# Splitting the first load of an expert half and scaling its second step's rows on VectorE

## The chip, the cores and the metric

The kernel runs on one core of one Trainium2 chip. The metric is the device time of one launch in microseconds (us). Before the change it is 1599.24 us, the median of three runs.

## What is computed

The reference is one layer of three residual blocks on an input `x` of 2 sequences, 4096 tokens each, 256 wide: half of a mixture-of-experts feed-forward block (FFN), an attention block of the delta-rule kind, and half of the same FFN again, each on a layer norm of `x`.

```python
x = x + 0.5 * ffn(layernorm(x))
x = x + attention(layernorm(x))
x = x + 0.5 * ffn(layernorm(x))

def ffn(x, gate_w, w1, w2, w3):          # 8192 tokens, 8 experts, width 256, hidden 128
    scores = softmax(x @ gate_w)
    top_scores, top_idx = top_k(scores, 2)
    scale = zeros((T, E)).at[arange(T)[:, None], top_idx].set(top_scores)
    xs = scale.T[:, :, None] * x[None]
    h = silu(einsum('etd,edh->eth', xs, w1)) * einsum('etd,edh->eth', xs, w3)
    return einsum('eth,ehd->etd', h, w2).sum(axis=0)
```

## The kernel before

`build` calls `ffn`, `attention` and `ffn` again. Both FFNs run the same expert code. A token goes to two experts, so the work is done in two **halves**: the first half takes every token to its best expert, the second to its second best. The tokens of a half lie in a list in device memory (`rows1`, named first_rows in the trace, then `rows2`, named second_rows), sorted by expert. A row of the first list holds the token (256 floats) and 6 floats (goal, factors, addends): 1048 bytes. A row of the second list has 256 floats more ahead of them, the token plus half of the first expert's answer (the **sum part**): 2072 bytes. The remaining 262 floats are called the **token part** here.

A half has 18 **steps** (`NSP`), numbered `start` to `end - 1`, so there are 36 steps in an FFN (`NST`) and the second half starts at step 18. A step is 4 tiles of 128 rows, each with one expert. The queues are these, and their order is the order of the code:

- SyncE (SP) loads rows: `load_rows(k)` at L360 to L368 reads four row addresses from a table in SBUF with `table_row` (L345, a TENSOR_LOAD and registers), then issues four transfers, each with an address instruction ahead of it. There are 8 row buffers `xw[k % 8]`. At step 18 it first waits until every store of the first half has landed, since those stores write the list that it now reads.
- ScalarE (ACT) in `scaled(k)` (L752) multiplies the step's rows by their factors and adds the addends, one instruction for a tile, into `xs[k % 2]` (a view of ffn_xb in the trace). `high_part(k)` (L759) rounds the turned rows, `silu(k)` is L764, `high_hidden(k)` L769.
- TensorE (PE) turns the rows with `turn_rows(k)` (L457, 8 matmuls), multiplies them with two expert matrices in `up(k)` (L468, 24 matmuls), turns the hidden values (`turn_hidden`, L481) and multiplies down (`down`, L491).
- VectorE (DVE) casts the goals (`goals(k)`, L652), makes the low part of the turned rows (`low_part(k)`, L657), multiplies the hidden values (`hidden`, L662), makes their low part (`low_hidden`, L667), and adds half of the answer (`results`, L673).
- GpSimd (POOL) stores the rows of a step by indirect transfers, one for a tile (`put`, L829).

`up(k)` needs both parts of the turned rows of its step, and stands on TensorE's queue behind `turn_rows(start + 1)` in the first step of a half. What comes before the first `silu` of a half is called its **head** here. There are four heads: H1 and H2 in the first FFN (starting at 133.88 and 260.27 us), H3 and H4 in the second (1336.16 and 1462.25 us).

Of the kernel before, what the change touches and what calls it, by code (L numbers as in the profile page):

```python
# [6 lines left out]
P = 128  # L7
# [202 lines left out]
def ffn(nc, name, src, rows1, rows2, sums, kept, fresh, first_stage):  # L210
# [13 lines left out]
    with ctx:  # L224
# [3 lines left out]
        def sem(n):  # L228
            return kept.semaphore(f"{name}_{n}")

        def sems(n, k):
            return [sem(f"{n}{j}") for j in range(k)]
# [70 lines left out]
        def pt(n, shape):  # L303
# [19 lines left out]
        scattered = sems("scattered", 4)  # L323
        tab_step, tab_ready, filled = sem("tab_step"), sem("tab_ready"), sems("filled", 2)
        row_loaded, stored, xs_ready = sems("row_loaded", NW), sems("stored", NW), sem("xs_ready")
        (to_ready, tr_done, xhi_ready, xlo_ready, up_done, sil_ready, hid_ready, hT_done, hhi_ready, hlo_ready,
         down_done, y_ready) = (sem(n) for n in (
             "to_ready", "tr_done", "xhi_ready", "xlo_ready", "up_done", "sil_ready", "hid_ready", "hT_done",
# [22 lines left out]
        def _(sp):  # L351
# [4 lines left out]
            def load_rows(k):  # L356

                if k >= NW:
                    sp.wait_ge(stored[k % NW], 16 * TPB * (k // NW))
                if k == NSP:  # L360
                    for b in range(NW):
                        sp.wait_ge(stored[b], 16 * TPB * ((NSP + NW - 1 - b) // NW))
                    sp.wait_ge(filled[1], 16 * E)
                for j, r in enumerate(table_row(k, 1, mybir.EngineType.SP, NROWS - P)):
                    if k < NSP:
                        sp.dma_start(xw[k % NW][:, j, DM:], rows1[bass.ds(r, P)]).then_inc(row_loaded[k % NW], 16)  # L366
                    else:
                        sp.dma_start(xw[k % NW][:, j], rows2[bass.ds(r, P)]).then_inc(row_loaded[k % NW], 16)  # L368
# [38 lines left out]
        def _(pe):  # L407
# [39 lines left out]
                          start=False, stop=True, skip_group_check=True).then_inc(pos_done, 1)  # L447

            def turn_rows(k):
                pe.wait_ge(xs_ready, k + 1)  # L450
                if k == 0 and first_stage:
                    pe.wait_ge(xT_ready, 2 * NG)
                wait(pe, xhi_ready, k)
                wait(pe, xlo_ready, k)
                for j in range(TPB):
                    for q in range(KC):
                        last = pe.transpose(tr[:, q, j * P:(j + 1) * P], xs[:, k % 2, j, q * P:(q + 1) * P], ident[:])  # L457
                last.then_inc(tr_done, 1)
# [74 lines left out]
        def _(dve):  # L533
# [114 lines left out]
            def goals(k):  # L648
# [2 lines left out]
                wait(dve, stored[k % NW], 16 * TPB * (k // NW))  # L651
                dve.tensor_copy(to[:, k % NW], xw[k % NW][:, :, 2 * DM + 5 if k < NSP else 2 * DM]).then_inc(to_ready, 1)  # L652

            def low_part(k):
                dve.wait_ge(xhi_ready, k + 1)
                wait(dve, up_done, k - 1)
                dve.tensor_tensor(xlo[:, k % 2], tr, xhi[:, k % 2].bitcast(F32), ALU.subtract).then_inc(xlo_ready, 1)  # L657
# [11 lines left out]
            def results(k):  # L669
                for h in range(2):  # L670
                    two = slice(2 * h, 2 * h + 2)
                    dve.wait_ge(down_done, 2 * k + h + 1)
                    dve.scalar_tensor_tensor(xw[k % NW][:, two, 0:DM], yb[:, two], 0.5,  # L673
                                             xw[k % NW][:, two, DM:2 * DM] if k < NSP else xw[k % NW][:, two, 0:DM],
                                             ALU.mult, ALU.add).then_inc(y_ready, 1)
# [32 lines left out]
                split_low(NG - 1)  # L708

            for start, end in HALVES:  # L710
                goals(start)
                low_part(start)
                goals(start + 1)
# [14 lines left out]
        def _(act):  # L728
# [59 lines left out]
            for start, end in HALVES:  # L788
                scaled(start)
                high_part(start)  # L790
                scaled(start + 1)
                high_part(start + 1)
                scaled(start + 2)
                for k in range(start, end):
                    silu(k)
                    if k + 2 < end:
# [1524 lines left out]
```

## Time and profile before

| | us |
|---|---|
| three runs | 1593.64, 1599.24, 1599.90 |
| their median | 1599.24 |
| the profiled execution's own time | 1593.92 |
| its span, from the first to the last instruction | 1592.2 |

| engine | busy us | share of the span |
|---|---|---|
| TensorE matmul | 1325.0 | 83% |
| TensorE weight load | 1241.4 | 78% |
| VectorE | 1119.1 | 70% |
| GpSimd | 998.5 | 63% |
| ScalarE | 918.2 | 58% |

The profile is of one execution. Busy shares are means over stages with different limits: the steady part of a half keeps TensorE busy all the time, and a head leaves it idle. So a change to the heads is read in the four heads, in the timeline and in the chain of waits, and not in the shares.

### The profile page before, as it was taken

To read this page: it belongs to the slowest core of one execution; us is meant where nothing else is said; L and a number is where in the kernel's file an instruction comes from. 1 tells how busy PE (TensorE), PEld (TensorE's weight loads), DVE (VectorE), ACT (ScalarE), POOL (GpSimd) and SP (SyncE) were. 2 spreads that over 40 slices of the span, in tenths; PEclk is the share of its full clock that TensorE was granted. 3 is DMA by queue.
4 is the path that set the end of the run, shared out by engine and by line. 5 is a ranking of instruction groups with operands and counts; after the bars stand their busy time and mean duration, and the time that the engine had idled before them with its cause. 6 is when DMAs were issued, how large, how long until landed. Compare 5 with 4: busy or idle time off the path is not lost. (4 is left out here: it accounts for less than half of the span.)

```text
span 1592.2 us, 36649 instructions
## 1 busy us (share of the span) xinstructions
PE 1325.0 (83%) x11688; PEld 1241.4 (78%) x11688; DVE 1119.1 (70%) x2788; ACT 918.2 (58%) x1853; POOL 998.5 (63%) x1812
## 2 busy tenths in 40 slices
PE   7773994994589999999999999999999841995996
PEld 7663994994478888888888888888888741994996
DVE  6574772673768788879888888797887534673674
ACT  2123772771356676767676767676767423772773
POOL 4772673575366676777776867877768532575466
PEclk8556996998789999999999999999999965997999
DMA  7437976672011212132222231322222245875792
GB/s 212 154 108 190 312 256 223 233 252 69 11 30 39 51 46 75 40 74 76 63 67 58 62 77 35 79 72 67 68 56 62 62 143 157 267 265 190 251 291 75
DMA packets 224024, 195.88 MB, mean 123 GB/s; under 512 B 105556, under 2 KB 186714, under 8 KB 223840
## 3 DMA queue, kind: packets, MB, share of 16 engines
q1 hardware_dynamic: 190560, 117.21, 26.8%
q0 software_dynamic: 24576, 67.94, 11.7%
q10 hardware_dynamic: 8704, 8.39, 1.8%
q8 instruction: 102, 1.67, 0.5%
q14 instruction: 82, 0.67, 0.1%
HBM read 103.68 MB, written 96.10 MB: 125 GB/s over the span
## 5 line engine op out<-in xcount | busy, mean ns | idle before, releaser
L1557 DVE SCALAR_TENSOR_TENSOR raw_w<-attn_raw,taps,raw_w 128x256 f32<-128x256 f32 x576 | 249.0, 491 | 58.6 <-ACT raw_w L1928 58.6
L468 PE MATMUL ffn_both<-ws,ffn_xhi 128*128 x1152 | 204.3, 289 | 0.4
L468 PEld LDWEIGHTS ffn_both<-ws,ffn_xhi 128*128 128x128 f32 x1152 | 164.8, 192 | 2.8 <-issue 2.8
L457 PE MATMUL ffn_both<-ident,ffn_xb 128*128 128x128 f32 x576 | 82.0, 290 | 94.7 <-ACT ffn_xb L752 94.7
L2210 POOL TENSOR_TENSOR attn_inv<-attn_inv,attn_term 64x14 f32<-64x14 f32 (+6 forms) x448 | 136.5, 305 | 35.1
L2207 POOL TENSOR_TENSOR attn_term<-attn_small,attn_inv 64x14 f32<-64x14 f32 (+6 forms) x448 | 131.1, 293 | 32.6
L1199 PE MATMUL attn_fr<-attn_xhi,wqkv 128*128 128x256 f32 x768 | 148.0, 295 | 2.5 <-DVE attn_xlo L1537 1.6
L457 PEld LDWEIGHTS ffn_both<-ident,ffn_xb 128*128 128x128 f32 x576 | 70.1, 150 | 97.1 <-ACT ffn_xb L752 76.9
L491 PE MATMUL ffn_yb<-ws,ffn_hhi 128*128 x576 | 119.9, 292 | 6.2 <-DVE ffn_hlo L667 6.2
L1199 PEld LDWEIGHTS attn_fr<-attn_xhi,wqkv 128*128 128x128 f32 x768 | 112.5, 193 | 14.1 <-issue 10.6
L829 POOL DMA_INDIRECT second_rows<-ffn_more_rows,ffn_to x64 | 63.1, 986 | 85.3 <-DVE ffn_to L652 69.3
L468 PE MATMUL ffn_both<-ws,ffn_xlo 128*128 x576 | 116.1, 283 | 0.0
L657 DVE TENSOR_TENSOR ffn_xlo<-ffn_both,ffn_xhi 128x1024 fp32r<-128x1024 f32 x72 | 87.7, 1218 | 37.0 <-ACT ffn_xhi L759 36.8
L662 DVE TENSOR_TENSOR ffn_hid<-ffn_both,ffn_sil 128x512 f32<-128x512 f32 x72 | 49.8, 691 | 88.8 <-ACT ffn_sil L764 88.8
L752 ACT ACTIVATE ffn_xb<-ffn_more_rows 128x256 f32<-128x256 f32 x120 | 62.1, 591 | 79.0 <-DMA ffn_more_rows<-first_rows 44.0
L491 PEld LDWEIGHTS ffn_yb<-ws,ffn_hhi 128*128 128x128 f32 x576 | 94.5, 191 | 7.2 <-issue 7.2
L764 ACT ACTIVATE ffn_sil<-ffn_both 128x512 f32<-128x512 f32 x72 | 43.0, 597 | 91.0 <-PE ffn_both L468 91.0
L759 ACT ACTIVATE ffn_xhi<-ffn_both 128x1024 fp32r<-128x1024 f32 x72 | 73.9, 1026 | 34.0 <-PE ffn_both L457 34.0
L468 PEld LDWEIGHTS ffn_both<-ws,ffn_xlo 128*128 128x128 f32 x576 | 90.0, 191 | 0.0
L2150 POOL DMA_INDIRECT first_rows<-attn_xg,attn_slots x64 | 66.8, 1043 | 36.6 <-issue 17.1
L818 POOL DMA_INDIRECT first_rows<-ffn_xb,ffn_slots x64 | 65.0, 1016 | 36.8 <-DVE ffn_xb L642 18.9
L1928 ACT ACTIVATE raw_w<-attn_raw,taps 128x256 f32<-128x256 f32 x192 | 86.7, 498 | 1.6
(317 smaller groups left out, 4051.1 us busy)
## 6 DMA issues: line engine op xcount, KB each, us to landing
ffn_more_rows<-second_rows SPq DMA_DIRECT2D x56, 259.0 KB
ffn_xb<-second_rows SPq DMA_DIRECT2D x48, 259.0 KB
raw_w<-second_rows SPq DMA_DIRECT2D x40, 259.0 KB
ffn_more_rows<-first_rows SPq DMA_DIRECT2D x64, 131.0 KB
ffn_xb<-in_L_attn_x_dram SPq DMA_DIRECT2D x8, 1024.0 KB, 5.9
attn_xin<-x_after_first ACTq DMA_DIRECT2D x32, 256.0 KB, 2.7
attn_xres<-x_after_first SPq DMA_DIRECT2D x32, 256.0 KB, 3.0
x_after_attention<-attn_xres SPq DMA_DIRECT2D x32, 256.0 KB
```

What stands on the lines that cost most here:

```text
L457: last = pe.transpose(tr[:, q, j * P:(j + 1) * P], xs[:, k % 2, j, q * P:(q + 1) * P], ident[:])
L468: last = pe.matmul(hp[:, j, :], (xhi, xlo)[b][:, k % 2, q, j * P:(j + 1) * P], ws[:, bass.ds(experts[j], 1), a, q].rearrange("p o d -> p ( ...
L491: last = pe.matmul(yb[:, j, :], (hhi, hlo)[b][:, k % 2, j * P:(j + 1) * P], ws[:, bass.ds(experts[j], 1), a, 2].rearrange("p o d -> p (o d)"),
L657: dve.tensor_tensor(xlo[:, k % 2], tr, xhi[:, k % 2].bitcast(F32), ALU.subtract).then_inc(xlo_ready, 1)
L759: act.activation(xhi[:, k % 2], tr, ACT.Copy).then_inc(xhi_ready, 1)
L818: pool.indirect_dma_start(out=rows1, out_offset=bass.IndirectOffsetOnAxis(ap=slots[:, m % 2, j:j + 1], axis=0), in_=xb[:, m % 4, j, :], in ...
L1199: last = pe.matmul(out, w[:, a, q, col], (xhi, xlo)[b][:, q, :], skip_group_check=True, start=(start and k == 0 and q == 0), stop=(k == 2 ...
L1557: dve.scalar_tensor_tensor(acc[:, j, r], raw[:, j, r, :, tap:tap + P], taps[:, j, r, tap:tap + 1], acc[:, j, r], ALU.mult, ALU.add)\
L1928: act.activation(acc[:, j, r], raw[:, j, r, :, 0:P], ACT.Copy, scale=taps[:, j, r, 0:1])\
L2150: pool.indirect_dma_start(out=rows1, out_offset=bass.IndirectOffsetOnAxis(ap=slots[:, j:j + 1], axis=0), in_=xg[:, j, :], in_offset=None). ...
L2207: pool.tensor_tensor(term[:, 0:k, 0:j], n[:, j + 1:, j:j + 1].broadcast_to([BP, k, j]), v[:, j:j + 1, 0:j].broadcast_to([BP, k, j]), ALU.m ...
L2210: pool.tensor_tensor(v[:, j + 1:, 0:j], v[:, j + 1:, 0:j], term[:, 0:k, 0:j], ALU.subtract)\
```

## The change

It touches `ffn` alone, and so both FFNs.

1. ScalarE no longer scales the rows of the second step of a half (`start + 1`). It scales those of `start` and, behind `high_part(start)`, those of `start + 2`.
2. VectorE scales them, in the new `second_scaled`, ahead of `goals(start)` and `low_part(start)` on its queue. TensorE waits for the new semaphore `xs_second` in that step.
3. At step 18 SyncE reads its addresses before it waits for the stores, and loads the rows in two parts: the four token parts first, then the four sum parts with a semaphore of their own (`sum_loaded`). The first `results` of the second half waits for that one.

```diff
@@ load_rows(k), SyncE
                 if k >= NW:
                     sp.wait_ge(stored[k % NW], 16 * TPB * (k // NW))
+                places = table_row(k, 1, mybir.EngineType.SP, NROWS - P)
                 if k == NSP:
+                    sp.wait_ge(filled[1], 16 * E)
                     for b in range(NW):
                         sp.wait_ge(stored[b], 16 * TPB * ((NSP + NW - 1 - b) // NW))
-                    sp.wait_ge(filled[1], 16 * E)
-                for j, r in enumerate(table_row(k, 1, mybir.EngineType.SP, NROWS - P)):
+                    for j, r in enumerate(places):
+                        sp.dma_start(xw[k % NW][:, j, DM:], rows2[bass.ds(r, P), DM:]).then_inc(row_loaded[k % NW], 16)
+                    for j, r in enumerate(places):
+                        sp.dma_start(xw[k % NW][:, j, 0:DM], rows2[bass.ds(r, P), 0:DM]).then_inc(sum_loaded, 16)
+                    return
+                for j, r in enumerate(places):
@@ turn_rows(k), TensorE
-                pe.wait_ge(xs_ready, k + 1)
+                if k in (1, NSP + 1):
+                    pe.wait_ge(xs_second, 1 if k == 1 else 2)
+                else:
+                    pe.wait_ge(xs_ready, k + 1 - (k > 1) - (k > NSP + 1))
@@ VectorE
+            def second_scaled(k):
+                dve.wait_ge(row_loaded[k % NW], 16 * TPB * (k // NW + 1))
+                if k == 1 and first_stage:
+                    wait_scattered(dve)
+                wait(dve, tr_done, k - 1)
+                c = 2 * DM + 1 if k < NSP else 2 * DM + 3
+                for j in range(TPB):
+                    row = xw[k % NW][:, j]
+                    last = dve.tensor_scalar(xs[:, k % 2, j], row[:, DM:2 * DM], row[:, c:c + 1], row[:, c + 1:c + 2],
+                                             ALU.mult, ALU.add)
+                last.then_inc(xs_second, 1)
@@ results(k), VectorE
                     dve.wait_ge(down_done, 2 * k + h + 1)
+                    if k == NSP and h == 0:
+                        dve.wait_ge(sum_loaded, 16 * TPB)
@@ the loop over the halves, VectorE
             for start, end in HALVES:
+                second_scaled(start + 1)
                 goals(start)
                 low_part(start)
@@ the loop over the halves, ScalarE
                 scaled(start)
                 high_part(start)
-                scaled(start + 1)
+                scaled(start + 2)
                 high_part(start + 1)
-                scaled(start + 2)
```

SyncE's queue at step 18 of the first FFN, where the second half starts. Before:

```order
L345 TENSOR_LOAD tab [waits ffn1_stored4,ffn1_stored5,ffn1_stored3,ffn1_stored6,ffn1_stored2,ffn1_stored7,ffn1_stored1,ffn1_filled1,ffn1_stored0]
L368 ISA
L368 DMA ffn_more_rows<-second_rows 128x518
...
L345 TENSOR_LOAD tab [waits ffn1_stored3]
...
L368 DMA raw_w<-second_rows 128x518
```

After (each DMA row stands for four, with an ISA or REGISTER_ALU row ahead of each):

```order
L346 TENSOR_LOAD tab [waits ffn1_stored2]
L367 ISA [waits ffn1_stored4,ffn1_stored3,ffn1_stored5,ffn1_stored2,ffn1_stored6,ffn1_stored1,ffn1_stored7,ffn1_stored0,ffn1_filled1]
L367 DMA ffn_more_rows<-second_rows 128x262
...
L369 REGISTER_ALU
L369 DMA ffn_more_rows<-second_rows 128x256
...
L346 TENSOR_LOAD tab [waits ffn1_stored3]
...
L375 DMA raw_w<-second_rows 128x518
```

The address read moved ahead of the wait for the stores, and four more transfers stand ahead of the loads of step 19 (into raw_w).

ScalarE's queue in the head of that half, before:

```order
L752 ACTIVATE ffn_xb<-ffn_more_rows 128x256 [waits ffn1_tr_done,ffn1_row_loaded2]
L759 ACTIVATE ffn_xhi<-ffn_both 128x1024 [waits ffn1_up_done,ffn1_tr_done]
L752 ACTIVATE ffn_xb<-raw_w 128x256 [waits ffn1_tr_done,ffn1_row_loaded3]
...
L759 ACTIVATE ffn_xhi<-ffn_both 128x1024 [waits ffn1_up_done,ffn1_tr_done]
L752 ACTIVATE ffn_xb<-raw_w 128x256 [waits ffn1_tr_done,ffn1_row_loaded4]
```

and after:

```order
L777 ACTIVATE ffn_xb<-ffn_more_rows 128x256 [waits ffn1_tr_done,ffn1_row_loaded2]
L784 ACTIVATE ffn_xhi<-ffn_both 128x1024 [waits ffn1_up_done,ffn1_tr_done]
L777 ACTIVATE ffn_xb<-raw_w 128x256 [waits ffn1_tr_done,ffn1_row_loaded4]
...
L784 ACTIVATE ffn_xhi<-ffn_both 128x1024 [waits ffn1_up_done,ffn1_tr_done]
L789 ACTIVATE ffn_sil<-ffn_both 128x512 [waits ffn1_hid_ready,ffn1_up_done]
```

The scaling of step 19 (row_loaded3) left this queue, and the second rounding now stands behind the scaling of step 20 (row_loaded4).

VectorE's queue in the first head, after the change; before it, the same rows stood without the two of L672:

```order
L672 TENSOR_SCALAR ffn_xb<-ffn_more_rows 128x256 [waits ffn1_scattered2,ffn1_scattered1,ffn1_scattered3,ffn1_scattered0,ffn1_row_loaded1]
L672 TENSOR_SCALAR ffn_xb<-ffn_more_rows 128x256 x3
L662 CAST ffn_to<-ffn_more_rows 128x4 [waits ffn1_row_loaded0]
L679 TENSOR_TENSOR ffn_xlo<-ffn_both,ffn_xhi 128x1024 [waits ffn1_xhi_ready]
L662 CAST ffn_to<-ffn_more_rows 128x4 [waits ffn1_row_loaded1]
L679 TENSOR_TENSOR ffn_xlo<-ffn_both,ffn_xhi 128x1024 [waits ffn1_xhi_ready]
```

The low part of the first step (the first L679) now stands behind four scalings that wait for the second step's rows.

## Rows read from the trace of the kernel before

**Rows 1.** Chain of waits, head H4: start us, us, what.

```profile
1459.54 2.10 DMA second_rows<-ffn_more_rows,ffn_to
1462.25 0.33 SPq L368
...
1463.80 3.72 DMA ffn_more_rows<-second_rows
...
1472.59 2.07 ACT ffn_xb L752 x4
1474.71 1.97 PE ffn_both L457 x8
1476.68 4.04 PE ffn_both L468 x24
```

**Rows 2.** Chain of waits, steady part of the last half, two steps.

```profile
1499.73 2.83 PE ffn_both L468 x24
...
1505.29 2.83 PE ffn_both L468 x24
```

**Rows 3.** Timeline of the last half, GpSimd's first store of a step.

```profile
1494.63 0.98 POOL L829 DMA_INDIRECT out_dram<-raw_w,ffn_to  x1 [0.69 <-DVE ffn_to L652]
```

**Rows 4.** Timeline, head H3 (start us, us, engine, line, operation).

```profile
1336.16 6.98 SPq L366 DMA_DIRECT2D ffn_more_rows<-first_rows  x12
...
1340.23 2.07 ACT L752 ACTIVATE ffn_xb<-ffn_more_rows 128x256 f32<-128x256 f32 x4 [23.20 <-DMA ffn_more_rows<-first_rows]
1342.36 1.97 PE L457 MATMUL ffn_both<-ident,ffn_xb 128*128 128x128 f32 x8 [29.52 <-ACT ffn_xb L752]
...
1345.42 1.22 DVE L657 TENSOR_TENSOR ffn_xlo<-ffn_both,ffn_xhi 128x1024 fp32r<-128x1024 f32 x1 [5.02 <-ACT ffn_xhi L759]
...
1349.02 0.78 PE L468 MATMUL ffn_both<-ws,ffn_xhi 128*128 x2
...
1353.88 0.60 ACT L764 ACTIVATE ffn_sil<-ffn_both 128x512 f32<-128x512 f32 x1 [0.19 <-PE ffn_both L468]
```

**Rows 5.** Timeline, head H1.

```profile
133.88 7.24 SPq L366 DMA_DIRECT2D ffn_more_rows<-first_rows  x12
137.60 2.07 ACT L752 ACTIVATE ffn_xb<-ffn_more_rows 128x256 f32<-128x256 f32 x4 [20.29 <-DMA ffn_more_rows<-first_rows]
...
142.96 1.23 DVE L657 TENSOR_TENSOR ffn_xlo<-ffn_both,ffn_xhi 128x1024 fp32r<-128x1024 f32 x1 [5.19 <-ACT ffn_xhi L759]
...
146.56 0.78 PE L468 MATMUL ffn_both<-ws,ffn_xhi 128*128 x2
...
149.89 0.40 PE L468 MATMUL ffn_both<-ws,ffn_xhi 128*128 x2
149.96 1.28 ACT L764 ACT_TABLE_LOAD   x1
```

**Rows 6.** Lines by form: VectorE, the nearest operation to the new scaling.

```profile
L1530 DVE TENSOR_SCALAR attn_xn<-attn_xin,attn_mv,attn_rstd 128x256 f32<-128x256 f32 x64 | 25.2, 433 | 1.2 <-POOL attn_rstd L2133 1.2
```

**Rows 7.** Windows (stretch, us, PE, PEld, DVE, ACT, POOL, PEclk, DMA share, GB/s).

```profile
1351.40:1353.70 2.30, 2.30 (x16) 2.30 (x16) 0.29 (x1) 2.28 (x4) 0.00 (x0) 0.67 0.81 222
...
1476.70:1478.70 2.00, 2.00 (x11) 2.00 (x11) 0.93 (x1) 1.99 (x4) 0.00 (x0) 0.50 1.05 397
...
146.90:148.90 2.00, 2.00 (x15) 2.00 (x14) 0.90 (x1) 1.95 (x4) 0.00 (x0) 0.72 0.88 264
```

**Rows 8.** Timeline, head H4: SyncE's loads of steps 19 and 20, and the low part.

```profile
1464.65 4.63 SPq L368 DMA_DIRECT2D raw_w<-second_rows  x8
...
1472.73 1.22 DVE L657 TENSOR_TENSOR ffn_xlo<-ffn_both,ffn_xhi 128x1024 fp32r<-128x1024 f32 x1 [5.02 <-ACT ffn_xhi L759]
```

**Rows 9.** Timeline, head H2.

```profile
260.27 1.94 SPq L368 DMA_DIRECT2D ffn_more_rows<-second_rows  x4
...
266.24 2.07 ACT L752 ACTIVATE ffn_xb<-ffn_more_rows 128x256 f32<-128x256 f32 x4 [17.79 <-DMA ffn_more_rows<-second_rows]
...
273.40 1.97 PE L457 MATMUL ffn_both<-ident,ffn_xb 128*128 128x128 f32 x8 [3.07 <-ACT ffn_xb L752]
```

More of the change, by code:

```diff
@@ L325, in ffn @@
         row_loaded, stored, xs_ready = sems("row_loaded", NW), sems("stored", NW), sem("xs_ready")
+        sum_loaded, xs_second = sem("sum_loaded"), sem("xs_second")
         (to_ready, tr_done, xhi_ready, xlo_ready, up_done, sil_ready, hid_ready, hT_done, hhi_ready, hlo_ready,
```

## Prediction

> **What bounds the kernel now.** I read the chain of waits first. In the steady part of a half it runs through TensorE: `up` comes back after 5.56 us, from 1499.73 to 1505.29 [rows 2]. GpSimd has room there, since it waits 0.69 us for the next step's stores [rows 3]. So a half is a head plus steps at TensorE's pace, and what a head gains reaches the end of the program.
>
> In a head the chain leaves TensorE. H4 shows it best [rows 1]: the last store lands at 1461.64 (1459.54 + 2.10), SyncE issues its first load at 1462.25, the fourth at 1463.80 lands 3.72 us later. ScalarE scales the first step's rows, TensorE turns them, ScalarE rounds them, and only at 1472.59 does ScalarE scale the second step's rows, for 2.07 us. TensorE turns these from 1474.71 for 1.97 us and starts `up` at 1476.68. But `up` of the first step had its last input when VectorE finished the low part, at 1473.95 (1472.73 + 1.22) [rows 8]. The 2.7 us between are a detour: work of the second step ahead of the first step's `up`. H3 has the same pattern, low part ready at 1346.64 and `up` from 1349.02 [rows 4], and so has H1, 144.19 and 146.56 [rows 5].
>
> **The new scaling.** It is four tensor_scalar of 128x256 f32 with two operands per partition. L1530 has that very form and takes 433 ns [rows 6], so 4 x 0.433 = 1.7 us, in place of ScalarE's 2.07 us. It stands on VectorE ahead of the first low part, so that one waits until the second step's rows have landed and been scaled.
>
> The Trainium skill speaks of a shorter time: by "VectorE: DVE Perf Modes", section on the perf-mode tier table, a tensor_scalar on fp32 in SBUF runs at twice the plain rate. By that page an estimate is 0.3 us for each of the four, and the sum would be 10.5 us and not 9.5 us. The row above does not agree with it for this form, and I go by the row.
>
> **H3 and H1, first halves (loads unchanged).** In H3 twelve loads are issued in 6.98 us [rows 4], in three groups of four. A group takes 1.9 us [rows 9], so groups start 2.55 us apart. The first is landed at 1340.23, the second then at 1342.8. Scaled, it is ready at 1344.5, just as the first turning ends (1344.33). TensorE turns it until 1346.5. The low part is not delayed: its input is there at 1345.42, and it is ready at 1346.64. So `up` starts at 1346.7, 2.3 us sooner than 1349.02. In H1 a group comes every 2.65 us (12 in 7.24 us) after 137.60: the second lands at 140.25, is ready at 142.0 and turned by 144.0; low part at 144.19; `up` from 144.3, 2.3 us sooner than 146.56 [rows 5].
>
> Two things add to that. First, in H1 the table load for silu lasts until 151.24, while `up` was over at 150.29 (149.89 + 0.40) [rows 5]: 1 us of waiting. ScalarE now comes to the table load sooner. Third group landed at 142.9, scaled 142.95 to 145.0, second rounding to 146.0, table load to 147.3: 3.9 us sooner. Second, TensorE's clock. In the heads it was granted 0.5 (the 1.2 GHz level) and rose to the 2.4 GHz level within `up`: 0.67 on the mean over 1351.40 to 1353.70, 0.72 over 146.90 to 148.90 [rows 7]. Before, the engine idled 3.07 us between the two turnings; now they follow each other in H1 and H3. The rise may come earlier with that, or it may come when it came, and then more of `up` is slow. 24 matmuls take 2.83 us at the high level [rows 2], and 5.1 to 5.7 us at the low one (8 turnings take 1.97 us, 0.25 each with the fill, 0.21 without it). From 1346.7, `up` in H3 ends between 1349.6 and 1351.8, against 1353.88 before: 2.1 to 4.2 us gained. I take 3.4, since TensorE is now busy for 4 us before `up`. In H1 silu comes between 147.3 (table load) and 149.4, against 151.24: 1.8 to 3.9 us, and I take 3.2.
>
> **H4 and H2, second halves.** Reading the addresses early takes the TENSOR_LOAD out from between the last landing and the first issue. The gap was 0.61 us (1461.64 to 1462.25) and an address instruction stays, so I take 0.45 us, between 0.1 and 0.6. First issue: 1461.8. Four token parts are as large as the first halves' rows, which had landed 3.72 us (H1) and 4.07 us (H3) after their first issue [rows 4, 5]. Whole rows took 5.27 us in H4 (1462.25 to 1467.52) and 5.97 us in H2 (260.27 to 266.24) [rows 1, 9]. So the first step's rows are there at 1465.7, 1.8 us sooner, and they are turned by 1469.8.
>
> But the second step's rows now stand behind eight transfers and not four. Their first issue was 2.4 us after the first step's (1462.25 to 1464.65 [rows 8]). Four more at 0.52 us each (1463.80 less 1462.25, over three) make it 4.5 us: 1466.3. Four whole rows need 5.3 to 6.0 us, so they land at 1471.6 to 1472.3. VectorE scales them until 1473.3 to 1474.0, against 1474.66 for ScalarE before. So this gains 1.4 to 0.7 us and not 2.7: the second step's rows are the **new wait**, and little of the split load's 1.8 us is left on the path. I take 1.1 in H4. In H2 the same sum (260.27 - 0.45 + 4.5 + 5.3 to 6.0, plus 1.7) gives 271.3 to 272.0, against 273.40 [rows 9]: 2.1 to 1.4 gained, and I take 1.8. The clock does as before here, since TensorE still idles some 3.5 us between the turnings.
>
> Behind the new wait stands the low part of step 18, ready at 1474.5 to 1475.2. Step 19's turning ends at 1475.3 to 1476.0, so it costs nothing. On ScalarE the second rounding stands behind the scaling of step 20. The transfers run at their limit in this stretch (DMA share 1.05, 397 GB/s [rows 7]); a step's 1.06 MB take 2.7 us, so step 20 lands by 1475.0, is scaled by 1477.1, step 19 rounded by 1478.1, its low part done by 1479.4. The second `up` needs that at about 1481.7, so 2.3 us cover it; without that cover it would cost its excess in H2 and H4. The sum parts are needed by `results` some 15 us later: nothing. In steady steps nothing changes on any engine, and GpSimd's queue is not touched.
>
> **Sum.** 3.2 (H1) + 1.8 (H2) + 3.4 (H3) + 1.1 (H4) = 9.5 us. The low ends give 1.8 + 1.4 + 2.1 + 0.7 = 6.0; the high ends 3.9 + 2.1 + 4.2 + 1.4 = 11.6. Against the profiled execution's own 1593.92 us the forecast is 1584.4. The median of the runs shown is 5.3 us higher, 1599.24, from where it is 1589.7. Single runs lie at either level, so I give 1588.
>
> **The rivals.**
> - *The low sum.* The slow clock eats the first halves' gain: `up` starts sooner, but all of it runs at 1.2 GHz. For it: in H3 the clock rose only at about 1352.9, long after the second turning began. Against it: in H1 it rose 3 us after. 6 us less than the median is 1593, no change to a measurement. 30%.
> - *VectorE is quicker at the scaling.* Its 1.22 us for 1024 elements against 0.433 for 256 give 0.16 us and 1.03 ns for each element. At half of that, four take 1.2 us, 0.5 us sooner in H4 and H2 each: 10.5 us in all, 1587. That is the tier table's case in the Trainium skill's "VectorE: DVE Perf Modes". 10%.
> - *Slower: VectorE stuck at the second step's rows.* The place is the start of the second halves, where the low part and `up` wait for loads behind eight transfers. It decides once step 19's rows land later than 1474.66 - 1.7 = 1472.9; each us beyond is paid in H4 and H2. Were they served in turn with the sum parts and with step 20, they would carry 1.4 + 2.7 us more and land at about 1476: 3 us lost in each. With the first halves at their low ends (3.9 us) that is 2 us slower, 1601, and more if their own issue is held up too. Against it: step 18's rows landed 5.3 us after issue with step 19's right behind them. 7%.
> - *The change does not do what it says*: the early address read could itself wait, for the store of its buffer (stored2). That store is older than the last one by several steps. 3%, at a price of 0.9 us.
>
> **How the numbers follow.** What can be told from no change is about 0.5%, 8 us. My forecast has 50% and the quicker VectorE 10%; they pass 8 us in most cases, though runs lie 6 us apart. The low sum has 30% and seldom passes. Faster by over 0.5%: 0.55; within: 0.40; slower: 0.05. The range goes from 1581.4 (1593.92 less 11.6 and the quicker VectorE's 1.0) to 1597, which takes in the low sum with a median of 1599 to 1603 before.
>
> **What the changed profile would show.** Scalings of 0.43 us on VectorE; `up` of H3 at 1346.7 and its silu at about 1350.4; H1's table load at 146; in H4 the first issue 0.15 us after the last landing, the first step's rows 3.9 us after it and the second step's 10 us after it, and TensorE idle for some 3.5 us between the two turnings. I am wrong if scaling in H4 or H2 starts more than 11 us after the first issue, if `up` lasts over 4.6 us in H1 or H3, or if a steady step is longer than 5.56 us.

## The result, and the profile after

| | before | after |
|---|---|---|
| median of 20 runs each, us | 1598.01 | 1594.95 |
| lowest and highest | 1593.64, 1602.43 | 1591.90, 1598.32 |
| ratio, with its 95% interval | | 0.9982 [0.9974, 0.9991] |
| the profiled execution, its span | 1593.92, 1592.2 | 1596.45, 1594.3 |

By the ratio the change makes the kernel 2.9 us faster (1.4 to 4.2): a gain, but 0.18% and not the 0.6% of the forecast. The two profiled executions stand the other way round. What differs between them is mostly code that the change doesn't touch: H1 begins at 137.86 us after and at 133.88 before [rows 5], and over the other traces of this study it begins anywhere from 132.98 to 143.62. So the spans say nothing about 3 us, and I compare heads, each from its own start.

The timeline of H3 after the change, PE's `up` cut after its first piece (start us, us, engine, line, operation, idle before and what ended it):

```profile
1338.71 6.72 SPq L373 DMA_DIRECT2D ffn_more_rows<-first_rows  x12
1342.45 2.07 ACT L777 ACTIVATE ffn_xb<-ffn_more_rows 128x256 f32<-128x256 f32 x4 [20.49 <-DMA ffn_more_rows<-first_rows]
...
1344.58 1.97 PE L467 MATMUL ffn_both<-ident,ffn_xb 128*128 128x128 f32 x8 [27.12 <-ACT ffn_xb L777]
1345.37 1.38 DVE L672 TENSOR_SCALAR ffn_xb<-ffn_more_rows 128x256 f32<-128x256 f32 x4 [12.13 <-DMA ffn_more_rows<-first_rows]
...
1347.64 1.23 DVE L679 TENSOR_TENSOR ffn_xlo<-ffn_both,ffn_xhi 128x1024 fp32r<-128x1024 f32 x1 [0.81 <-ACT ffn_xhi L784]
...
1349.01 1.94 PE L467 MATMUL ffn_both<-ident,ffn_xb 128*128 128x128 f32 x8 [2.46 <-DVE ffn_xlo L679]
...
1350.60 0.78 PE L478 MATMUL ffn_both<-ws,ffn_xhi 128*128 x2
...
1355.54 0.60 ACT L789 ACTIVATE ffn_sil<-ffn_both 128x512 f32<-128x512 f32 x1 [2.23 <-PE ffn_both L478]
```

It answers to [rows 4]. VectorE has the second step's rows scaled at 1346.75, 0.2 us after the first turning is over. TensorE could turn them then, and I had forecast just that. It idles 2.46 us from the end of the first turning, and what releases it is the low part of the first step. That is the finding of this case: **the second turning needs the first low part**, although it reads none of it.

Of H4, to be held against [rows 1, 8]:

```profile
1463.96 1.92 SPq L367 DMA_DIRECT2D ffn_more_rows<-second_rows  x4
1466.07 1.84 SPq L369 DMA_DIRECT2D ffn_more_rows<-second_rows  x4
1467.71 2.07 ACT L777 ACTIVATE ffn_xb<-ffn_more_rows 128x256 f32<-128x256 f32 x4 [15.27 <-DMA ffn_more_rows<-second_rows]
1468.45 4.40 SPq L375 DMA_DIRECT2D raw_w<-second_rows  x8
...
1474.34 1.38 DVE L672 TENSOR_SCALAR ffn_xb<-raw_w 128x256 f32<-128x256 f32 x4 [17.56 <-DMA raw_w<-second_rows]
...
1475.71 1.22 DVE L679 TENSOR_TENSOR ffn_xlo<-ffn_both,ffn_xhi 128x1024 fp32r<-128x1024 f32 x1
...
1477.07 1.94 PE L467 MATMUL ffn_both<-ident,ffn_xb 128*128 128x128 f32 x8 [5.27 <-DVE ffn_xlo L679]
```

and the chain of waits through the same head (start us, us, what):

```profile
1461.59 2.09 DMA second_rows<-ffn_more_rows,ffn_to
...
1470.01 4.31 DMA raw_w<-second_rows
...
1474.69 1.03 DVE ffn_xb L672 x3
...
1475.80 1.14 DVE ffn_xlo L679
...
1477.07 1.94 PE ffn_both L467 x8
1479.01 3.78 PE ffn_both L478 x24
```

The first step's rows are there 3.75 us after the first issue (before: 5.27), but the chain doesn't pass through them any more. It goes through the last load of step 19, the scaling, and only then the low part, whose input had been there since about 1472.9 (ScalarE's rounding, 1471.84 + 1.02). H2 is the same, with the second step's rows another 1.0 us later:

```profile
263.38 1.95 SPq L367 DMA_DIRECT2D ffn_more_rows<-second_rows  x4
...
267.23 2.07 ACT L777 ACTIVATE ffn_xb<-ffn_more_rows 128x256 f32<-128x256 f32 x4 [15.35 <-DMA ffn_more_rows<-second_rows]
...
274.72 1.38 DVE L672 TENSOR_SCALAR ffn_xb<-raw_w 128x256 f32<-128x256 f32 x4 [19.55 <-DMA raw_w<-second_rows]
...
277.45 1.94 PE L467 MATMUL ffn_both<-ident,ffn_xb 128*128 128x128 f32 x8 [6.13 <-DVE ffn_xlo L679]
```

The table has every trace of the study (the experiments follow). The first four columns are the us from the start of a head to its first `up` matmul. The clock plays little part in them, since the turnings ahead of it take 1.94 or 1.97 us in the traces of before and after alike. A head starts with its first load's issue in H1 and H3, and with the last store's start in H2 and H4, so that SyncE's wait counts. "To silu" is the sum over the four heads up to the first silu, with the clock's luck in it.

| kernel | H1 | H2 | H3 | H4 | sum | to silu |
|---|---|---|---|---|---|---|
| before | 12.68 | 17.44 | 12.86 | 16.79 | 59.8 | 78.1 |
| e9_before_again | 13.00 | 17.11 | 12.69 | 17.71 | 60.5 | 79.1 |
| after | 12.11 | 18.03 | 11.89 | 17.08 | 59.1 | 77.6 |
| e1_after_again | 12.27 | 18.07 | 11.91 | 17.02 | 59.3 | 76.4 |
| e8_after_third | 12.07 | 17.42 | 11.93 | 16.57 | 58.0 | 73.7 |
| e2_dve_only | 12.59 | 16.71 | 12.28 | 16.35 | 57.9 | 76.3 |
| e10_dve_only | 12.34 | 16.52 | 11.94 | 16.90 | 57.7 | 74.9 |
| e3_split_only | 13.00 | 17.06 | 12.47 | 16.08 | 58.6 | 78.3 |
| e11_split_only | 12.95 | 16.82 | 12.62 | 16.43 | 58.8 | 76.9 |
| e4_low_first | 12.29 | 16.77 | 11.98 | 15.68 | 56.7 | 73.6 |
| e5_second_psum | 10.63 | 15.72 | 10.34 | 16.22 | 52.9 | 69.6 |
| e6_tokens_first | 12.26 | 14.63 | 12.14 | 14.60 | 53.6 | 70.3 |
| e7_both | 10.88 | 13.28 | 10.43 | 12.75 | 47.3 | 60.6 |
| e12_both | 10.73 | 13.18 | 10.33 | 12.75 | 47.0 | 63.6 |

So in H1 and H3 `up` starts 0.6 and 1.0 us sooner than in the profile of before, and in H2 and H4 0.6 and 0.3 us later. One kernel's traces differ too, by up to 0.9 us in H4 (16.79 and 17.71 for the kernel before). On the mean of the traces of both programs H1 and H3 gain 0.7 and 0.9 us, H2 loses 0.6 and H4 gains 0.4, so the 0.3 us of H4 are not to be read. Steady steps are as they were. The chain of after, last half:

```profile
1501.87 2.83 PE ffn_both L478 x24
1507.43 2.83 PE ffn_both L478 x24
```

5.56 us apart, as in [rows 2]. The mean of three traces of this program, against two of before, is 1.4 us less to `up` and 2.7 us less to silu, which goes with the measured 2.9 us but does not prove it, as 77.6 and 73.7 for one program show.

### The profile page after: what moved, and what is told of

It reads as the page before. It is cut to its first block and busy times, and to the rows that moved or that the text cites. A ratio compares the mean times of both kernels' runs of the same rounds, so it can differ in the third digit from the quotient of the medians.

```text
span 1594.3 us, 36675 instructions
## 1 busy us (share of the span) xinstructions
PE 1327.1 (83%) x11688; PEld 1243.2 (78%) x11688; DVE 1124.8 (71%) x2804; ACT 910.7 (57%) x1837; POOL 996.9 (63%) x1812
## 5 line engine op out<-in xcount | busy, mean ns | idle before, releaser
L679 DVE TENSOR_TENSOR ffn_xlo<-ffn_both,ffn_xhi 128x1024 fp32r<-128x1024 f32 x72 | 87.7, 1218 | 17.1 <-ACT ffn_xhi L784 17.1
L777 ACT ACTIVATE ffn_xb<-ffn_more_rows 128x256 f32<-128x256 f32 x112 | 58.0, 591 | 71.8 <-DMA ffn_more_rows<-first_rows 41.1
```

## The experiments

Where the wait comes from stands in the code, unchanged by the diff. `turn_rows(k)`, and TensorE's queue for step 1 (its second turning) after the change:

```python
                wait(pe, xhi_ready, k)
                wait(pe, xlo_ready, k)
                for j in range(TPB):
                    for q in range(KC):
                        last = pe.transpose(tr[:, q, j * P:(j + 1) * P], xs[:, k % 2, j, q * P:(q + 1) * P], ident[:])
```

```
L467 MATMUL ffn_both<-ident,ffn_xb 128x128 [waits ffn1_xlo_ready,ffn1_xhi_ready,ffn1_xs_second]
```

There is one turning buffer, `tr`, a half of `both` in PSUM. ScalarE rounds from it and VectorE makes the low part from it, so it is free for step k + 1 only when both have read step k. In the traces of before this wait never shows, since ScalarE's scaling ended later still: in [rows 4] the low part is ready at 1346.64, and the second turning starts 0.8 us after it, released by ScalarE's scaling:

```profile
1347.40 1.97 PE L457 MATMUL ffn_both<-ident,ffn_xb 128*128 128x128 f32 x8 [3.07 <-ACT ffn_xb L752]
```

**Theory A**, the turning buffer: this wait took the gain, in all four heads, and in H2 and H4 VectorE's scaling of the late rows stands ahead of it too. Theory A also expects nothing or a small loss from the split load by itself, since it makes step 19's rows late. **Theory B**, its rival, says that the first result's 2.9 us are a real gain of the heads that will show again, and that the split load carries it. Two of the three batches ran on chips on which the same program takes 7.5 to 8.5% longer (last section), so each ratio is against runs of the kernel before on the same chip.

### First batch: the parts apart

The parts, each in a kernel with the other undone. `e2_dve_only` has the loads of before:

```diff
 load_rows(k), SyncE, against after
-                places = table_row(k, 1, mybir.EngineType.SP, NROWS - P)
                 if k == NSP:
-                    sp.wait_ge(filled[1], 16 * E)
                     for b in range(NW):
                         sp.wait_ge(stored[b], 16 * TPB * ((NSP + NW - 1 - b) // NW))
...
+                    sp.wait_ge(filled[1], 16 * E)
+                for j, r in enumerate(table_row(k, 1, mybir.EngineType.SP, NROWS - P)):
```

`e3_split_only` has the new loads, and ScalarE scales the second step as before:

```diff
 the loops over the halves, against after
-                second_scaled(start + 1)
...
-                scaled(start + 2)
+                scaled(start + 1)
                 high_part(start + 1)
+                scaled(start + 2)
```

`e4_low_first` puts the low part ahead of the scaling in H2 and H4 alone, where the rows come late:

```diff
-                second_scaled(start + 1)
+                if start == 0:
+                    second_scaled(start + 1)
                 goals(start)
                 low_part(start)
+                if start > 0:
+                    second_scaled(start + 1)
```

`e1_after_again` is the changed kernel itself.

> The changed kernel itself, beside its parts. Theory A (the turning buffer): the second turning of a half overwrites the PSUM buffer that the first low part still reads, so in H1 and H3 it moves up only from ScalarE's 2.07 us to that low part, 0.7 to 0.9 us each, and in H2 and H4 it is held by VectorE's wait for step 19's rows, which costs 0 to 1.1 us each. Then the whole is 0 to 1.5 us faster than before. Theory B: the first result (2.9 us faster) is a real gain of the heads, and comes back here at 2 to 4 us.

Measured: 0.9993 [0.9970, 1.0017] against 1733.57 us before, 1.2 us faster with an interval from 5.2 faster to 2.9 slower: it can't be told from no change, and its interval takes in both theories. `up` starts as in the first trace, within 0.2 us in each head.

> Parts 1 and 2 alone (VectorE scales the second step's rows), loads as before. Theory A: H1 and H3 gain 0.7 to 0.9 us each as in the whole change. In H2 and H4 step 19's rows land 8 to 9 us after the first issue, before the first low part's input is there, so VectorE waits for nothing: there too the second turning starts right behind the first low part, 0.7 us sooner than before. Sum 2.5 to 3 us faster than before, more than the whole change. Theory B (the split load carries the gain): under 1.5 us faster.

Measured: 0.9978 [0.9963, 0.9993], 3.8 us faster, on Theory A's side. In H2 and H4 step 19's rows land sooner (four transfers ahead of them and not eight), and `up` comes 1.4 and 0.7 us before that of e1. They land 9.3 to 9.4 us after the first issue, later than the 8 to 9 us expected.

> Part 3 alone (split load and early addresses), ScalarE scales all rows as before. Theory A: H1 and H3 as before. In H2 and H4 the first step's rows are there some 2 us sooner after the last landed store, but ScalarE then waits for step 19's rows (11 us after the first issue) and scales them for 2.07 us, so the second turning starts 0 to 2 us later than before: no change to 3 us slower in the sum. Theory B: 1.5 to 3 us faster.

Measured: 0.9999 [0.9976, 1.0021], 0.2 us faster with an interval from 4.2 faster to 3.6 slower. The time lies where Theory A had it, but its reason does not hold: it had the second turning 0 to 2 us later than before, and `up` in H2 and H4 comes 0.4 and 0.7 us sooner than in the profile of before. The trace shows no loss from the split alone. ScalarE is free when step 19's rows land, and the low part is done at 1581.74, 1.9 us before the scaling is (1583.65), as the timeline of H4 shows:

```profile
1577.45 1.97 PE L464 MATMUL ffn_both<-ident,ffn_xb 128*128 128x128 f32 x8 [13.04 <-ACT ffn_xb L761]
1579.46 1.02 ACT L768 ACTIVATE ffn_xhi<-ffn_both 128x1024 fp32r<-128x1024 f32 x1 [2.06 <-PE ffn_both L464]
1580.52 1.22 DVE L664 TENSOR_TENSOR ffn_xlo<-ffn_both,ffn_xhi 128x1024 fp32r<-128x1024 f32 x1 [5.02 <-ACT ffn_xhi L768]
...
1581.58 2.07 ACT L761 ACTIVATE ffn_xb<-raw_w 128x256 f32<-128x256 f32 x4 [1.10 <-DMA raw_w<-second_rows]
```

The low part runs beside the waiting for the rows and their scaling. In the changed kernel it runs after both.

> The changed kernel, but in the second halves VectorE makes the first low part before it scales the second step's rows. Theory A: the low part (1.22 us) leaves the path between step 19's rows and the second turning in H2 and H4, so it is 1.2 us per head, 2.4 us in all, faster than the changed kernel. Theory C (the turning waits for the rows anyway, low part hidden): no difference to the changed kernel.

Measured: 0.9970 [0.9950, 0.9990], 5.2 us faster. `up` starts 1.3 us sooner in H2 and in H4 than in e1 (18.07 to 16.77, 17.02 to 15.68), as expected from taking one low part of 1.22 us off the path. Its H4:

```profile
1581.19 1.23 DVE L679 TENSOR_TENSOR ffn_xlo<-ffn_both,ffn_xhi 128x1024 fp32r<-128x1024 f32 x1 [5.02 <-ACT ffn_xhi L787]
...
1582.55 1.38 DVE L672 TENSOR_SCALAR ffn_xb<-raw_w 128x256 f32<-128x256 f32 x4
...
1583.99 1.97 PE L467 MATMUL ffn_both<-ident,ffn_xb 128*128 128x128 f32 x8 [3.89 <-DVE ffn_xb L672]
```

By the traces this is the better order for the second halves. The times alone don't show it: the four intervals of this batch overlap, and the four medians lie within 1.2 us of each other (1731.16, 1730.54, 1731.71 and 1730.95 for e1 to e4).

### Second batch: the buffer and the queue of loads

`e5_second_psum` turns the second step of a half into `yb`, the PSUM tensor of the answers, which nobody uses yet in a head. The wait for the first step's parts falls away because nothing is overwritten:

```diff
+        ty = yb[:].rearrange("p j d -> p (j d)").rearrange("p (c t) -> p c t", c=KC)
+        def side(k):
+            return ty if k in (1, NSP + 1) else tr
...
-                wait(pe, xhi_ready, k)
-                wait(pe, xlo_ready, k)
+                if k == NSP + 1:
+                    pe.wait_ge(y_ready, 2 * NSP)
+                back = 1 if k in (1, NSP + 1) else 0
+                wait(pe, xhi_ready, k - back)
+                wait(pe, xlo_ready, k - back)
...
-                        last = pe.transpose(tr[:, q, j * P:(j + 1) * P], xs[:, k % 2, j, q * P:(q + 1) * P], ident[:])
+                        last = pe.transpose(side(k)[:, q, j * P:(j + 1) * P], xs[:, k % 2, j, q * P:(q + 1) * P], ident[:])
```

The rounding and the low part read `side(k)` likewise.

> The changed kernel, but the second step of a half is turned into the PSUM tensor of the results (yb), which stands idle in a head, so its turning need not wait for the first low part. Theory A (that wait is the step that my prediction left out): in H1 and H3 the second turning starts right behind the first or behind VectorE's scaling, 2 to 2.5 us sooner than in the changed kernel, up follows right behind the low part, and the kernel is 4 to 5 us faster than the changed one; in H2 and H4 the turning starts behind the scaling of step 19 (1.2 us sooner each), 2 us more. Rival (the slow clock gives it back): up starts sooner but lasts longer, and under 3 us in all are gained.

Measured: 0.9959 [0.9938, 0.9981] against 1718.11 us before, 7.0 us faster (3.3 to 10.7). The timeline of H3:

```profile
1405.24 1.97 PE L474 MATMUL ffn_both<-ident,ffn_xb 128*128 128x128 f32 x8 [28.79 <-ACT ffn_xb L784]
1405.68 1.38 DVE L679 TENSOR_SCALAR ffn_xb<-ffn_more_rows 128x256 f32<-128x256 f32 x4 [13.44 <-DMA ffn_more_rows<-first_rows]
...
1407.12 1.97 PE L474 MATMUL ffn_yb<-ident,ffn_xb 128*128 128x128 f32 x8
...
1408.31 1.23 DVE L686 TENSOR_TENSOR ffn_xlo<-ffn_both,ffn_xhi 128x1024 fp32r<-128x1024 f32 x1 [1.17 <-ACT ffn_xhi L791]
1409.78 0.79 PE L485 MATMUL ffn_both<-ws,ffn_xhi 128*128 x2 [0.70 <-DVE ffn_xlo L686]
```

Now the second turning does follow the first directly, it starts before the low part, and `up` starts when that is done, which is the picture of the prediction. `up` comes 1.4 and 1.6 us sooner in H1 and H3 than in e8, the changed kernel on the same chip. The second turning itself starts 2.6 to 2.7 us sooner, a little more than expected, but `up` still waits for the low part. By the two ratios e5 is 3.7 us faster than e8, a little less than the 4 to 5 us expected.

Sooner is not yet shorter. Windows of `up` in H1 and in H3 of this one trace (stretch, us, PE, PEld, DVE, ACT, POOL, PEclk, DMA share, GB/s):

```profile
148.63:151.10 2.47, 2.46 (x21) 2.47 (x21) 0.78 (x1) 2.45 (x4) 0.00 (x0) 1.00 0.86 234
...
1409.78:1412.28 2.50, 2.50 (x11) 2.50 (x12) 1.01 (x1) 2.48 (x4) 0.00 (x0) 0.50 0.76 212
1412.28:1415.00 2.72, 2.72 (x17) 2.72 (x16) 0.22 (x1) 0.26 (x1) 0.00 (x0) 0.59 0.81 215
```

In H1 it ran at the 2.4 GHz level throughout and lasted 3.1 us; in H3 at the 1.2 GHz level for its first half and 5.2 us in all. That is the "low sum" of the rivals in one head and its opposite in the other.

`e6_tokens_first` leaves `tr` alone and changes the order of the loads: the token parts of steps 18, 19 and 20 first, then step 21, then the three groups of sum parts.

```diff
-                    for j, r in enumerate(places):
-                        sp.dma_start(xw[k % NW][:, j, DM:], rows2[bass.ds(r, P), DM:]).then_inc(row_loaded[k % NW], 16)
...
+                    for n in range(3):
+                        for j, r in enumerate(more[n]):
+                            sp.dma_start(xw[(k + n) % NW][:, j, DM:], rows2[bass.ds(r, P), DM:])\
+                              .then_inc(row_loaded[(k + n) % NW], 16)
+                    load_rows(k + 3)
+                    for n in range(3):
+                        for j, r in enumerate(more[n]):
+                            sp.dma_start(xw[(k + n) % NW][:, j, 0:DM], rows2[bass.ds(r, P), 0:DM])\
+                              .then_inc(sum_loaded, 16)
```

> The changed kernel, but at step 18 SyncE issues the token parts of steps 18, 19 and 20 first, then the rows of step 21, and only then the sum parts of the three. Theory A: step 19's token parts land about 6 us after the first issue and not 11, so VectorE scales before the first low part's input is there; the second turning in H2 and H4 starts right behind the low part, at 9.5 to 10 us after the first issue and not 13 to 14. 3.5 us per head, 7 us faster than the changed kernel in all. Rival (transfers bound it): landing 8 us or later, under 3 us in all.

Measured: 0.9972 [0.9954, 0.9991], 4.8 us faster. Its H4:

```profile
1554.02 1.91 SPq L369 DMA_DIRECT2D ffn_more_rows<-second_rows  x4
...
1558.09 2.07 ACT L784 ACTIVATE ffn_xb<-ffn_more_rows 128x256 f32<-128x256 f32 x4 [15.39 <-DMA ffn_more_rows<-second_rows]
1560.20 1.38 DVE L679 TENSOR_SCALAR ffn_xb<-raw_w 128x256 f32<-128x256 f32 x4 [12.92 <-DMA raw_w<-second_rows]
...
1564.65 1.94 PE L474 MATMUL ffn_both<-ident,ffn_xb 128*128 128x128 f32 x8 [2.46 <-DVE ffn_xlo L686]
```

Step 19's rows land 6.2 us after the first issue, where it was 10.4 in the trace of after. Idle before the second turning is 2.46 us, as in H1 and H3 of the changed kernel: what is left is the buffer. Against e8 `up` comes 2.8 us sooner in H2 and 2.0 in H4. Expected were 3.5 us in each and 7 us in all; by the two ratios it is 1.5 us faster than e8. That is the size of the rival (under 3 us) without its reason, since the rows land at 6.2 and 6.5 us and not at 8 or later.

`e7_both` is e5 and e6 together, and `e8_after_third` the changed kernel again.

> Both of these together: second turning in the idle PSUM tensor, and token parts of three steps first. Theory A: the gains add, up starts 2.3 us sooner in H1 and H3 and over 4 us sooner in H2 and H4 than in the kernel before: 11 to 14 us faster than before (0.7 to 0.9%). Rival: a later wait (rows of step 21, or the clock) takes half of it.

Measured: 0.9942 [0.9920, 0.9965], 10.0 us faster (6.0 to 13.7), where 11 to 14 were expected.

> The changed kernel on the same chip as the three others, to compare them with. Theory A: 0 to 2 us faster than before; Theory B: 2 to 4 us faster.

Measured: 0.9981 [0.9964, 0.9998], 3.3 us faster (0.3 to 6.2), which repeats the first result's 0.9982. That is Theory B's range for the whole change, and more than Theory A gave it.

### Third batch: the same on a chip of the first kind

> The kernel before against itself: the width of no change, and a second trace of its four heads to compare with those of the variants on this chip. Both theories: ratio 1.000 within 0.002. Heads (from the first load issue in H1 and H3, from the start of the last store in H2 and H4, to the first silu) within 1 us of the first trace: 17.4, 21.8, 17.7, 21.2 us.

Measured: 1.0002 [0.9990, 1.0014] against 1597.21 us, so the comparison itself is true to 0.15%. Three heads are within 1 us of the first trace up to silu, as expected, but H4 took 22.6 us and not 21.2: one trace of a head is good to no better than 1.4 us up to silu.

> Second measurement of the VectorE part alone, beside the split load alone on the same chip. Theory A (low part frees the turning buffer): 2.5 to 4 us faster than before, as in the first measurement (0.9978); the second turning follows the first low part in all four heads.

Measured: 0.9994 [0.9979, 1.0009], 1.0 us faster, not to be told from none, where Theory A had 2.5 to 4. The second turning follows the first low part in all four heads, as it said, but the gain in time did not repeat.

> Second measurement of the split load alone. Theory A: within 1.5 us of the kernel before, either way, since step 19's rows land 11 us after the first issue and ScalarE takes them up later than before. Theory B: 1.5 us or more faster.

Measured: 0.9981 [0.9964, 0.9997], 3.0 us faster (0.5 to 5.7), on Theory B's side. In the first batch the two parts had 0.9978 and 0.9999, here 0.9994 and 0.9981: they changed places. So the times can't say which part is worth more. By the traces both bring `up` forward, the scaling 2.8 us over the four heads (e10 against e9), the split load 1.7 us (e11 against e9), and the whole change 1.2 to 2.5 us, less than the two added up. Each of these differences is of single traces, and so rough.

> Second measurement of the version with the second turning in the idle PSUM tensor and the token parts of three steps first. 9 to 13 us faster than before, clear of every other variant here.

Measured: 0.9933 [0.9915, 0.9952] over 6 runs, median 1586.67, 10.7 us faster (7.7 to 13.6). By its ratio it beats the kernel before and the change. Its chain through H4:

```profile
1460.75 1.97 PE ffn_yb L481 x8
1463.15 3.95 PE ffn_both L492 x24
```

and the timeline around it:

```profile
1458.66 1.97 PE L481 MATMUL ffn_both<-ident,ffn_xb 128*128 128x128 f32 x8 [14.81 <-ACT ffn_xb L791]
1459.31 1.38 DVE L686 TENSOR_SCALAR ffn_xb<-raw_w 128x256 f32<-128x256 f32 x4 [14.73 <-DMA raw_w<-second_rows]
...
1461.72 1.23 DVE L693 TENSOR_TENSOR ffn_xlo<-ffn_both,ffn_xhi 128x1024 fp32r<-128x1024 f32 x1 [0.95 <-ACT ffn_xhi L798]
```

The two turnings are back to back in all four heads, and `up` starts 2.3 to 5.0 us sooner than in e9.

**What follows.** Theory A's wait is shown. Giving the second turning its own buffer (e5) takes out the 2.46 us of idle time, and `up` moves by 1.4 and 1.6 us in the heads where no load is late. Against the two traces of before, `up` in e5's first halves starts 2.1 to 2.5 us sooner, which is the 2.3 us that the prediction had. In H2 and H4 both waits must go, the late rows (e6) and the buffer (e7, e12). In H2 `up` comes later with both parts of the change (17.42 to 18.07) than with either alone (16.52 to 17.06), and in H4 mostly (16.57 to 17.08 against 16.08 to 16.90). The traces show why: VectorE's low part stands behind the rows that the split made later, and with the low part first (e4) it is 16.77 and 15.68.

Theory A's sizes are not shown. The whole change was measured above the 0 to 1.5 us that it allowed in two comparisons of three (2.9 and 3.3, with intervals that reach down to 1.4 and 0.3), the scaling alone gained less in the third batch, and the split load did no harm. Whether the split load carries the gain, as Theory B has it, stays open by the times (0.2 and 3.0 us); by the traces it brings `up` forward by less than the scaling does.

One size stays open. Over the heads e12 is 15 us shorter than e9 up to silu, but the runs give 10.7; e5 is 9 us shorter than before and e6 8 us, where the runs give 7.0 and 4.8. Each trace is of one execution, and the clock in `up` differs between them. For e12 the choice of executions plays a part: the profiled ones took 1598.05 us (e9) and 1580.79 (e12, the fastest of its six), 17.3 us apart, and H1, ahead of which nothing was changed, begins at 139.02 and 132.98. So the 15 us are not to be taken for the size of the gain. How the rest divides was not found out.

## Why the prediction was wrong in size

Against its own steps:

- **The first halves: the step that failed.** "TensorE turns it until 1346.5. The low part is not delayed ... So `up` starts at 1346.7." The turning buffer was left out. The real chain of a first half is first turning, rounding, low part, second turning, `up`. From the low part's start to the second turning it is 1.37 us after and 1.98 before (ScalarE's scaling), so the step is worth 0.6 us in H1 and H3, not 2.3. The sum had 3.2 + 3.4 us for these two heads; up to `up` they gave 0.6 + 1.0, of which 0.3 in H3 is a first landing that came sooner (3.74 us after issue, 4.07 before), and up to silu 0.7 + 0.9. With the wait gone (e5) the 2.3 us up to `up` are there, so this term was wrong by the wait and not by the rest of its working.
- **The clock.** The 1 us or so added for an earlier rise rested on TensorE working for 4 us without a pause. It paused 2.46 us. `up` lasted 4.9 us in H3, where it was 4.8, and 4.5 in H1, where it was 3.7, at a mean granted clock of 0.64 against 0.81. So in H1 0.8 us of the 1 us that the table load gave back were lost again. That is luck of the execution: the kernel before itself has 3.7 and 4.9 us there in its two traces, at 0.81 and 0.58. The sign "over 4.6 us in H1 or H3" came, in H3, but it could tell nothing, since the profile of before had 4.8 there already. Even without the pause the rise isn't assured: e5 above has it both ways, and `up` lasts 3.1 to 5.2 us over all heads of all traces.
- **The low part in the second halves.** "Step 19's turning ends at 1475.3 to 1476.0, so it costs nothing." The same omission: the turning can't start before it. That is 1.35 us in each of H2 and H4 (1474.34 + 1.38 = 1475.72 to 1477.07), and e4, which undoes just that order, gets back 1.3 us in each. TensorE idles 5.27 us between the turnings in H4 and 6.13 in H2, where 3.5 were forecast. Of the 1.1 + 1.8 us that the sum had for H4 and H2 nothing shows up to `up`: 0.3 and 0.6 us later in the first pair of traces, 0.4 sooner and 0.6 later on the mean of all.
- **When step 19's rows land.** I forecast 9.8 to 10.5 us after the first issue. H4 has 10.4, H2 11.3, and over 11 was my own sign of being wrong. In H2 their first load was issued 4.9 us after step 18's first and not 4.5, which was H4's number, and the last landed 6.45 us later, where I had at most 6.0. The slower rival named this place and this point; its mechanism came in part, in H2, where `up` is 0.6 us later. The first halves outweighed it.
- **The new scaling.** Four take 1.38 us and not 1.7. A group's mean of one, 408 ns, is longer than the distance from one to the next, 0.35 us, since neighbours overlap. That could be read beforehand: L1530 has 64 instructions, 25.2 us busy and a mean of 433 ns [rows 6], but 64 x 0.433 is 27.7. Busy time over count, 0.39 us, was the better price. The Trainium skill's "VectorE: DVE Perf Modes", section on the perf-mode tier table, has tensor_scalar on fp32 in SBUF at twice the plain rate. From that I had an estimate of 0.3 us for one, on two rows of record times; at the plain rate the same rows give an estimate of 0.42 us. The trace does not agree with the page for this form, since a record has 408 ns. That the four took 1.38 us, nearer to the estimate's 1.2 than to my 1.7, comes from the overlap and is luck for that rival. It changed nothing that matters: 0.3 us in each of H2 and H4.
- **The early addresses.** The last landing to the first issue takes 0.28 us after (1463.68 to 1463.96) and took 0.61. So 0.33 us, within 0.1 to 0.6, where I took 0.45.
- **The first step's rows.** 3.75 us (H4) and 3.85 (H2) after the first issue, against a forecast of 3.9. Right.
- **What was said to cost nothing.** Steady steps at 5.56 us, the second low part covered in H4 (done at 1481.86, `up` over at 1482.8), the sum parts never waited for: right. H1's table load left the path (over at 152.67, `up` at 154.5), though not as early as forecast.

The direction was right, and the time, 1594.95, lies in the range, whose lower end should be 1581.3 by its own terms and not 1581.4. It also lies near the 1593 of the "low sum", but that is luck for that rival: it had `up` starting 2.3 us sooner in the first halves and all of it slow. What was wrong is the weight: the forecast gave "faster by over 0.5%" 0.55, and 0.18% came. Most of it goes back to one wait that stood in two lines of code: the 6.6 us of the first halves were 1.6, and the low part of the second halves was not free. The forecast's 2.9 us for the second halves failed by that and by the late rows of H2 together.

## What to carry to other kernels

A step moved forward needs its inputs and also its output buffer. Before giving the time of a wait that goes away, list every other wait of the instruction behind it, in the code or on its queue, and write beside each when it would be met: a trace names only the last of them, so the next one is invisible until it decides. And put work whose inputs may land late behind, not ahead of, work on the same engine that is ready.

## What the runs showed of the hardware

- **The same program on another chip was 7.5 to 8.5% slower.** The kernel before had medians of 1598.01 and 1597.21 us in the first comparison and the third batch, and 1733.57 and 1718.11 in the other two. The granted clock does not explain it (e5's profiled execution has a mean of 0.898, after's 0.901), nor do single instructions: the first `up` of a half and the loads take as long. There are stretches in which the engines slow down or stop for some us. In e1 they stand in the waits under releasers that the trace of after has not at all (engine, line, what it waited for: us in total, times, longest):

```profile
ACT ffn_sil L789 <- remote: 85.9, 23, 7.2
...
ACT ffn_hhi L794 <- remote: 48.4, 12, 5.6
```

  One of them, as a window of 2.75 us in a steady stretch (columns as above), where TensorE works for 0.40 us at the full clock:

```profile
216.68:219.43 2.75, 0.40 (x4) 0.20 (x2) 1.90 (x3) 0.00 (x0) 1.44 (x2) 1.00 0.52 199
```

  What the engines wait for there the profile does not say, and no run looked for it. It is why ratios were only formed on one chip.
- **What a second group of loads costs.** Step 19's rows, whole and behind eight transfers, landed 10.4 and 11.3 us after the first issue (9.9 to 11.4 with e1 and e8). As the second group of four token parts, in e6 and e12, they landed after 6.2 to 6.5 us. Of the 4.2 us between after and e6 in H4 and the 4.9 in H2, issue accounts for 2.4 in each (their first load is issued 4.5 and 4.9 us after step 18's first, in e6 2.1 and 2.5) and whole rows in place of token parts for 1.5 and 2.1 (5.27 and 5.97 us in [rows 1, 9], 3.75 and 3.85 after). The rest, 0.3 us, is not accounted for.
